# A grouped convolution computed by windows of 16 input places for 8 outputs in channel groups three and four of a fused kernel

## What is computed

```
out = conv1d(x, weight, padding=4, groups=4)      # x (128, 32, 512): 32 channels, 9 taps
out = out + (cond @ c_weight.T)[:, :, None] + bias[None, :, None]
y   = (silu(out @ W_gate.T) * (out @ W_up.T)) @ W_down.T    # 512 -> 1376 -> 512, fp32
return x + y
```

## Time and profile before

| | |
|---|---|
| median of three runs | 752.04 us (751.13 to 752.36) |
| the profiled execution | 751.72 us |
| its span in the profile | 749.9 us (1.8 us lie around it) |
| granted TensorE clock | 0.999 of full |
| busy: PE / DVE / ACT / POOL | 739.6 / 379.5 / 274.4 / 52.4 us |
| convolution of group three (during g = 1) | 229 to 327 us of the span |
| convolution of group four (during g = 2) | 405 to 503 us of the span |

### The profile page before, as it was taken

How to read it: one execution, slowest core, us unless ns; L and a number is a source line. 1 busy time by engine, 2 the same in 40 slices (tenths; PEclk the granted TensorE clock), 3 DMA queues, 4 the chain that set the end, 5 groups by cost and what they waited for, 6 DMA issues and landing times.

```text
span 749.9 us, 10087 instructions
## 1 busy us (share of the span) xinstructions
PE 739.6 (99%) x3375; PEld 602.4 (80%) x3375; DVE 379.5 (51%) x639; ACT 274.4 (37%) x521; POOL 52.4 (7%) x88
## 2 busy tenths in 40 slices
PE   7999999999999999999999999999999999999998
PEld 6778888878888888887888888887888888887886
DVE  3896766654765454436734545443753333334224
ACT  4565655543433233234322333324431332333221
POOL 4433323210000000000000000000000000000000
PEclk9999999999999999999999999999999999999999
DMA  6496578569977677765544866866443967775413
GB/s 186 114 317 239 187 273 281 186 226 327 354 268 247 216 222 219 197 205 159 167 135 171 282 202 193 244 194 180 162 133 106 312 190 196 194 193 172 141 29 112
DMA packets 115029, 152.37 MB, mean 203 GB/s; under 512 B 12482, under 2 KB 50530, under 8 KB 114978
## 3 DMA queue, kind: packets, MB, share of 16 engines
q1 hardware_dynamic: 114496, 151.51, 64.8%
q10 hardware_dynamic: 482, 0.21, 0.1%
HBM read 108.95 MB, written 34.34 MB: 191 GB/s over the span
## 4 chain that ended last, share of the span: by engine, by line
PE 94%; DVE 2%; DMA 1%; SPq 1%; issue 1%; ACT 1%; POOL 0%; POOLq 0%; DVEq 0%
PE bank L727 55%; PE bank L790 32%; PE bank L645 3%; PE bank L640 3%; SPq L344 1%; PE bank L683 1%; DVE hc_lo L1091 1%; DMA x_in<-in_x 1%; PE bank L606 1%; PE bank L654 1%; PE bank L665 0%; DMA stage<-g_all 0%; DVE g_all L1294 0%; DVE ring L1091 0%; DVE g_all L1192 0%
## 5 line engine op out<-in xcount | busy, mean ns | idle before, releaser
L727 PE MATMUL bank<-hc_hi,ring 128*128 128x512 f32 (+1 forms) x1204 | 374.0, 392 | 1.0 <-issue 1.0
L727 PEld LDWEIGHTS bank<-hc_hi,ring 128*128 128x128 f32 (+1 forms) x1204 | 221.4, 185 | 50.2 <-issue 1.4
L727 PE MATMUL bank<-hc_lo,ring 128*128 128x512 f32 (+1 forms) x602 | 234.8, 390 | 0.0
L790 PE MATMUL bank<-ring,g_hi 128*128 128x512 f32 (+1 forms) x704 | 218.6, 392 | 0.0
L790 PEld LDWEIGHTS bank<-ring,g_hi 128*128 128x128 f32 (+1 forms) x704 | 131.2, 188 | 28.1 <-DVE g_lo L1091 0.8
L859 ACT ACTIVATE mix<-bank 128x512 f32<-128x512 f32 (+1 forms) x129 | 76.7, 594 | 188.0 <-PE bank L727 188.0
L790 PE MATMUL bank<-ring,g_lo 128*128 128x512 f32 (+1 forms) x352 | 137.1, 390 | 0.0
L727 PEld LDWEIGHTS bank<-hc_lo,ring 128*128 128x128 f32 (+1 forms) x602 | 111.5, 185 | 25.8
L1091 DVE TENSOR_TENSOR g_lo<-g_all,g_hi 128x512 fp32r<-128x512 f32 (+1 forms) x88 | 60.4, 689 | 88.6 <-ACT g_hi L859 88.6
L859 ACT ACTIVATE g_hi<-g_all 128x512 fp32r<-128x512 f32 (+1 forms) x88 | 55.1, 629 | 114.1 <-PE bank L790 114.0
L1265 DVE TENSOR_TENSOR mix<-bank,mix 128x512 f32<-128x512 f32 (+1 forms) x43 | 29.7, 691 | 129.4 <-PE bank L727 129.4
(11 more groups left out here) (141 smaller groups left out, 468.7 us busy)
## 6 DMA issues: line engine op xcount, KB each, us to landing
ring<-saved SPq DMA_DIRECT2D x319, 256.0 KB, 3.0
saved<-ring SPq DMA_DIRECT2D x99, 256.0 KB, 3.7
g_all<-in_x SPq DMA_DIRECT2D x32, 256.0 KB, 3.6
out_y<-g_all SPq DMA_DIRECT2D x32, 256.0 KB, 3.7
x_in<-in_x SPq DMA_DIRECT2D x96, 64.0 KB, 2.1
stage<-win SPq DMA_DIRECT2D x96, 64.0 KB, 2.9
w_nat<-in_L_ffn_W_gate SPq DMA_DIRECT2D x10, 256.0 KB, 3.4
w_nat<-in_L_ffn_W_up SPq DMA_DIRECT2D x10, 256.0 KB, 3.4
```

Source lines behind the costliest of these rows:

```text
L727: mm = pe.matmul(bank[0:w, :], wt, hv, start=fresh and q == 0 and t == 0, stop=q == 1 and t == 2, skip_group_check=not fresh)
L790: mm = pe.matmul(acc(half, tt)[:], gs, wd, start=f == 0 and t == 0, stop=f == FC - 1 and t == 2)
```

## The change

For the groups three and four (`paired(grp)`, grp 2 and 3) the step is computed otherwise; the groups one and two stay as they are. The 128 rows that are contracted hold 16 neighbouring places of 8 channels, and with 9 taps 16 places suffice for 8 outputs of 8 channels, 64 columns of weights. The other 64 columns hold the `lo` part of the same weights. A step takes two windows, one shifted by 8 places, and multiplies each by [hi|lo] or [lo|hi] with the `hi` and the `lo` part of x: four matmuls of 128x512 into two banks, `conv_ps` and `xt_ps`. Afterwards DVE adds the two halves of 64 partitions of each bank. The tile `x_in` gets 8 places on both sides.

```diff
-        x_in = sb("x_in", [P, CG, P])
-        x_blk = sb("x_blk", [P, WB, R, CG])
+        x_in = sb("x_in", [P, CG, HALO + P + HALO])
+        x_turn = sb("x_turn", [P, 2 * WB * P])
...
+        pair_even, pair_odd = conv_t[:, 0:P], conv_t[:, HALF:HALF + P]
...
 # SP
+                    size = P + HALO if paired(grp) and i < KC - 1 else P
...
-                    if g + 1 < G and k == 2:
+                    soon = g + 1 < G and paired(g + 1)
+                    if g + 1 < G and k == (1 if soon else 2):
                         for kind in range(KINDS):
                             sp.wait_ge(hc_done[kind], hc_count(g, 1, kind))
-                    if g + 1 < G and 2 <= k < STEPS + 2:
+                    if g + 1 < G and 2 <= k < STEPS + 2 and not soon:
                         stage_step(g + 1, k - 2)
...
                     for fk in phase1[7 * f + 1:7 * f + 8]:
                         refill(product_at(g, *fk))
+                        if soon and fk[1] == K_S3 and 1 <= k <= STEPS:
+                            stage_step(g + 1, k - 1)
...
 # POOL
+            def pad_x(grp):
+                pool.wait_ge(x_turned, STEPS * grp + STEPS - 2)
+                pool.memset(x_in[:, :, HALO + P:], 0.0).then_inc(x_padded, 1)
...
+            pool.memset(x_in[:, :, 0:HALO], 0.0).then_inc(consts, 1)
             wrap(1)
...
 # PE
+                if paired(grp):
+                    for n, v in enumerate(xt(grp)):
+                        mm = pe.matmul(conv_ps[:, 0:P], pair_odd, v[:, 2 * WB * P:], start=n == 0, stop=n == 1)
...
+            def paired_step(grp, k):
+                pe.wait_ge(xt_lo_done, STEPS * grp + k + 1)
+                pe.wait_ge(conv_out, CPG * grp + k + 1)
+                for half, (bank, t) in enumerate(((conv_ps, pair_even), (xt_ps, pair_odd))):
+                    for n, v in enumerate(xt(grp)):
+                        mm = pe.matmul(bank[:], t, v[:, half * WB * P:(half + 1) * WB * P], start=n == 0, stop=n == 1)
+                mm.then_inc(conv_done, 1)
...
+                    if conv and k == 1 and paired(g + 1):
+                        conv_head(g + 1)
                     product(g, f, 1)
...
                     product(g, f, 2)
+                    if conv and 1 <= k <= STEPS and paired(g + 1):
+                        paired_step(g + 1, k - 1)
                     product(g, f, 3)
-                    if conv and 1 <= k <= STEPS:
+                    if conv and 1 <= k <= STEPS and not paired(g + 1):
                         conv_step(g + 1, k - 1)
...
 # ACT
+            def split_pairs(grp, k):
+                act.wait_ge(conv_done, CPG * grp + (k + 1 if k > 0 else 0))
+                act.wait_ge(x_turned, STEPS * grp + k + 1)
+                last = hi(xt_hi[:, 0:2 * WB * P], x_turn[:])
+                if k == 0:
+                    last = hi(xt_hi[:, 2 * WB * P:], head[:])
+                last.then_inc(xt_hi_done, 1)
...
                     copy_chain(n, f, 2)
                     silu_a(n, f)
+                    if conv and 0 <= k < STEPS and paired(g + 1):
+                        split_pairs(g + 1, k)
...
 # DVE
+                if paired(grp):
+                    if k == 0:
+                        dve.wait_ge(consts, 10)
+                        dve.transpose(head[:], x_in[:, :, 0:R].rearrange("p m (w r) -> p w m r", r=R))
+                    if k == STEPS - 1:
+                        dve.wait_ge(x_padded, grp - PAIRED + 1)
+                for half in range(2 if paired(grp) else 1):
+                    at = l0 + half * HALO
+                    last = dve.transpose(x_turn[:, half * WB * P:(half + 1) * WB * P],
+                                         x_in[:, :, at:at + WB * R].rearrange("p m (w r) -> p w m r", r=R))
...
+            def split_pairs(grp, k):
+                dve.wait_ge(xt_hi_done, STEPS * grp + k + 1)
+                last = lo(xt_lo[:, 0:2 * WB * P], x_turn[:], xt_hi[:, 0:2 * WB * P])
...
+            def read_pairs(grp, k):
+                i = k // 2
+                if k % 2 == 0:
+                    dve.wait_ge(staged[(i - 1) % KC], STAGED * (grp if i == 0 else grp + 1))
+                dve.wait_ge(conv_done, CPG * grp + k + 2)
+                lower, upper = slice(0, HALF), slice(HALF, P)
+                halves = ((conv_ps, lower, upper), (xt_ps, upper, lower))
+                w0 = k % 2 * WB
+                to = [windows(grp, i)[mine, w0:w0 + WB, :] for _, mine, _ in halves]
+                for n, (bank, mine, other) in enumerate(halves):
+                    dve.tensor_tensor(to[n], bank[other, :].rearrange("p (w n) -> p w n", w=WB),
+                                      ctxb[other, grp:grp + 1, :].broadcast_to([HALF, WB, P]), ALU.add).then_inc(conv_lo_out, 1)
+                for n, (bank, mine, other) in enumerate(halves):
+                    dve.wait_ge(conv_lo_out, (2 * STEPS + 2) * (grp - PAIRED) + 2 * k + n + 2)
+                    last = dve.tensor_tensor(to[n], bank[mine, :].rearrange("p (w n) -> p w n", w=WB), to[n], ALU.add)
...
-                    if conv and 0 <= k < STEPS:
+                    if conv and 0 <= k < STEPS and (k == 0 or not paired(g + 1)):
                         turn_x(g + 1, k)
+                    if conv and k == 1 and paired(g + 1):
+                        read_head(g + 1)
                     gate_a(n, f)
...
+                    if conv and 1 <= k <= STEPS and paired(g + 1):
+                        read_pairs(g + 1, k - 1)
                     if conv and 0 <= k < STEPS:
-                        split_x(g + 1, k)
+                        (split_pairs if paired(g + 1) else split_x)(g + 1, k)
...
                     up_b(n, f)
...
+                    if conv and 0 <= k < STEPS - 1 and paired(g + 1):
+                        turn_x(g + 1, k + 1)
                     up_a(n, f)
```

More of the change, by code:

```diff
@@ L132, in adaln_ffn, with paired @@
         toep = sb("toep", [P, G, QN, CG])
[L133 to L136, removed]
+        conv_t = sb("conv_t", [P, 4 * P], F32R)
         ident = sb("ident", [P, P])
         copy0, copy2, copy4, act_a, act_b = (mix[:, n, :] for n in range(5))
+        x_blk = x_turn[:, 0:WB * P].rearrange("n (b r c) -> n b r c", b=WB, r=R)
+        ta_hi, ta_lo, tb_hi, tb_lo = (conv_t[:, n * P:(n + 1) * P] for n in range(4))
+        PAIRED = 2
+        HALF = P // 2
+        pair_even, pair_odd = conv_t[:, 0:P], conv_t[:, HALF:HALF + P]
+        def paired(grp):
+            return grp >= PAIRED
         def down_nat(f):
@@ L296, in x_place @@
         def x_place(grp, i):
-            return x_first[:, i - 1] if grp == 0 and i > 0 else x_in[:]
+            return x_first[:, i - 1] if grp == 0 and i > 0 else x_in[:, :, HALO:HALO + P]
         def blocks(grp, k):
@@ L458, in _ @@
                     if g == 0 and f == FC - 2:
-                        for early in range(NDOWN):
-                            load_down(early)
+                        for fd in range(NDOWN):
+                            load_down(fd)
                     if g == 0 and f + 1 < FC:
@@ L561, in _ @@
                         mix_t_lo(f + 1)
+                    if g + 1 < G and paired(g + 1) and f == STEPS - 1:
+                        pad_x(g + 1)
         @block.tensor
@@ L827, in _ @@
                         turn_up(2)
-                    if conv and k == 1:
+                    if conv and k == 1 and not paired(g + 1):
                         conv_head(g + 1)
@@ L1053, in _ @@
                         split_toep(g + 1)
-                    if conv and 0 <= k < STEPS:
+                    if conv and 0 <= k < STEPS and not paired(g + 1):
                         split_x(g + 1, k)
@@ L1126, in split_toep @@
                     lo(t[2][:, R - HALO:, :], in_bank[0][:, 0:HALO, :], t[3][:, R - HALO:, :]).then_inc(t_lo_done, 1)
+                elif paired(grp):
+                    part = [conv_t[:, at:at + HALF].rearrange("p (q o) -> p q o", o=CG) for at in (0, HALF)]
+                    lo(part[1], toep[:, grp, HALO:2 * HALO, :], part[0]).then_inc(t_lo_done, 1)
                 else:
@@ L1136, in turn_x @@
                     dve.wait_ge(xt_lo_done, STEPS * grp + k)
-                l0 = k % 2 * WB * R
-                dve.transpose(x_turn, x_in[:, :, l0:l0 + WB * R].rearrange("p m (w r) -> p w m r", r=R)).then_inc(x_turned, 1)
+                l0 = HALO + k % 2 * WB * R
+                if paired(grp):
+                    if k == 0:
[7 more added lines that the diff above has]
+                                         x_in[:, :, at:at + WB * R].rearrange("p m (w r) -> p w m r", r=R))
+                last.then_inc(x_turned, 1)
+            def split_pairs(grp, k):
+                dve.wait_ge(xt_hi_done, STEPS * grp + k + 1)
+                last = lo(xt_lo[:, 0:2 * WB * P], x_turn[:], xt_hi[:, 0:2 * WB * P])
+                if k == 0:
+                    last = lo(xt_lo[:, 2 * WB * P:], head[:], xt_hi[:, 2 * WB * P:])
+                last.then_inc(xt_lo_done, 1)
             def split_x(grp, k):
```

(6 more changed lines are left out.)

26 lines of the change are left out of this document (18 added, 8 removed).

## The result

The changed kernel took 743.76 us as the median of five runs (742.70 to 743.95), the kernel before 752.04. The ratio is 0.9888, with a 95% interval of 0.9875 to 0.9902: 8.3 us faster. The forecast was 744.6 with a range of 743.9 to 748.5. The kernel before ran again beside the experiments, with medians of 751.65, 751.48 and 751.72 us; against these the gain is 7.7 to 8.0 us, so part of the 8.3 is scatter. The profiled execution took 743.76 us with a span of 742.0, 7.96 less than that of before.

What follows compares the result with a forecast made beforehand. PE was taken as the bound. Savings of 3.57 us a group, 7.14 us for two, came off the profiled 751.72 us, giving 744.58, predicted as 744.6; own range 743.9 to 745.6, up to 748.5 with most of rival 2 and some of 3.

Steps and rivals of the forecast that it cites:

- PE as the bound, a step paid in full: Chunks 7 to 9 of g = 1: PE is busy throughout, so a removed matmul saves its own time.
- The price of a matmul in the step: On PE, 0.228 us per matmul, from chunks with and without a step; two fewer save 0.455 us.
- Steps 0 to 6: Convolution steps on PE: six matmuls become four of the same size, saving 3.19 us for the seven.
- step 7: Last convolution step on PE: becomes four full matmuls, 1.19 us before and 0.91 after, saving 0.28 us.
- the head: Three PE matmuls of 128 columns, moved ahead of product 1, become two, saving 0.10 us.
- The passes of DVE: Four 64-partition passes ahead of `up_b`: 0.60 to 0.72 us each, 0.72 taken; slack before product 6 0.2 to 0.8 us.
- One argument beside it: On DVE, a pass price below 0.60 us has no ground: 96 and 128 partitions don't differ in the head's neighbours.
- The upper bound of 1.06: Highest price per DVE pass, from the slowest row, 4.24 us for four, in the start while POOL works.
- Rival 1: DVE passes of 1.06 us before `up_b` stall product 6 by 1.15 us, 14 times: 760.7 us; chance 0.08.
- Rival 2: Waits between dependent DVE passes add 0.1 to 0.2 us each; total 746.0 to 750.2 us; chance 0.12.
- Rival 3: Late staging holds `read_pairs` of steps 2, 4 and 6, costing 3 to 6 us: 747.5 to 750.6; chance 0.05.
- the staging in its own chunk: SP stages after the refill for product 4; landing at 9.3 to 11.2 us, before `read_pairs` at 11.6, costs nothing.

Runs made afterwards that it cites:

- the last experiment: The changed kernel with all four DVE passes reading the upper half of a bank and writing the lower half of a tile: 743.22 us in one execution.

## Why the prediction came out as it did

- **PE as the bound, a step paid in full: right.** PE is busy from end to end in the changed chunks. Two matmuls less shorten each chunk, and each of the two groups has its 3.85 us (group four alone: 747.76).
- **The price of a matmul in the step: too low, and this is the term that failed.** I took 0.228 from 9.58 us for 42 and found it again in 10.93 for 48. But 9.58 belongs to a chunk that has 0.06 us of its own on top; 9.52 is the bare one. By that the old step costs 1.41 us and not 1.35, and its matmuls 0.235 on average. Even that makes 0.47 for two. The runs with four and six matmuls show 0.49. An average was the wrong price: what leaves with the last two is also most of the slower pitch. Steps 0 to 6: 7 x 0.455 = 3.19 a group in my sum, 7 x 0.49 = 3.43 by those runs; step 7 saved 0.33 and not 0.28. Chunk 1, with its step and the head, saved 0.54, which leaves 0.05 for the head, not 0.10: its own matmuls went from 0.29 to 0.17 us, and the rest came back in a slower pitch behind them. The distances of g = 1 give 3.87 in all, and 2 x 0.29 us is the miss of the sum, 7.71 for 7.14.
- **The range: its lower end was too near.** 751.72 - 7.71 = 744.0, 0.1 above my lower end. I had given the forecast 0.7 us downward, for "the head and the run", while the three runs of before lay 1.2 us apart, and my sum started from yet another single execution. The rest of the way to 743.76 is in the start of the kernel, which scatters by 1 us from execution to execution. The five runs of the changed kernel lie 1.25 us apart themselves, and one of them (743.95) is within the range. So of the 0.82 us between sum and measurement 0.57 come from the price; that the median came out just below the range and not just inside it is chance.
- **The passes of DVE: right.** 0.72 us taken, 0.72 measured, 1.23 for the `lo`, and a slack of 0.14 us for 0.2. One argument beside it did not follow from its row: the neighbours of the head in the earlier trace rows both have 128 partitions, so they do not compare 96 with 128. The upper bound of 1.06, from the start with POOL at work, didn't come.
- **Rival 1** did not happen, but its mechanism is shown: with the step 1.36 us later PE stalls 14 times on `up_b`, and the kernel takes 760.57 us. The rival's 760.7 comes from a stall of about the same length, 1.15 us, brought about by slower passes, which no run shows. **Rival 2** neither: the waits between dependent passes cost nothing (the passes of the last experiment have them too, at 0.60).
- **Rival 3** was nearer than its chance of 0.05 says. The longest landing of a staging was 5.9 us (tile win), beyond the 4.8 of the earlier trace rows, and one transpose waited for `x_in` (the waits):

```profile
DMA to landing us min/median/max: 2.4/2.8/5.9
```

```profile
DVE x_turn L1204 <- DMA x_in<-in_x: 0.2, 1, 0.2
```

Neither reached PE. For the staging this was also luck of place: the 5.9 us were those of step 2 (issued at 268.87), and the next read that waits for a staging comes two chunks later. Had the staging of step 1 (last issue at 258.43) taken as long, it would have landed at 264.36, after the start of `read_pairs` at 263.98. That the staging in its own chunk costs nothing was right, and that it is needed is shown (750.68 without it).

- **Beside the sum:** I had not counted that the old step's second half waits for the next step's split. Before, it cost at most 0.04 us in a chunk. But with four matmuls in the old order it takes back 1.7 us; the new windows avoid that.

## What to carry to other kernels

**The price.** Take the price of a removed instruction from the difference of two stretches that differ in nothing else, and check the base on a third one; a base that has something of its own on top makes the saving too small.

**The deadline.** Where an engine's queue is in order, a change that adds work to a side engine is decided by one end time against one deadline in each period, here 5.99 us against 6.13, and not by its share of busy time (58% of DVE in the whole, while some 0.2 us more would have begun to cost the gain). And look one queue further: in three groups it was not DVE's own end but ACT's wait for DVE that PE felt, and with the old step behind product 4 a copy behind `split_x` on ACT.

## What the runs showed of the hardware

- Two matmuls of 128x512 at the end of a step of six cost 0.49 us, while the pitch elsewhere is 0.2267 us each. It depends on how many there are (chunks of 10.44 us with four, 10.93 with six, in either kernel). With six, the pitch stays at 0.228 to 0.236 us for the five matmuls behind the step, and the same is seen around a product whose weights have 96 columns in place of 128 (chunk 9: 9.58 us, the others 9.52). The cause is open.
- A pass of DVE that reads and writes other partitions than the one before starts 0.70 to 0.73 us behind it, one that reads and writes the same ones 0.60 to 0.61, for the same 0.69 us of duration. Reading one half of the partitions and writing the other costs nothing by itself.
